# Cross-attention keys of a four-layer network on one core: K written once in fp32, split into two fp16 parts by GpSimd

## The reference, cut to what matters

```python
# ctx' : L1 ada_ln(ctx), L2 layer norm of ctx, L3 ctx itself
k = (ctx' @ Wk + bk)            # 1500 x 128, 16 heads of 8
v = (ctx' @ Wv + bv)
scores = einsum('bhqd,bhkd->bhqk', q, k) * 8 ** -0.5
out = einsum('bhqk,bhkd->bqhd', softmax(scores), v)
```

## Time and profile before

| | us |
|---|---|
| median of 3 runs (lowest, highest) | 2066.11 (2053.47, 2067.04) |
| profiled execution | 2056.51 |
| its span in the trace | 2054.7 |
| busy in the span: PE, DVE, ACT, POOL | 1635.4, 1236.0, 1004.1, 422.9 |

### The profile page before, as it was taken

One profiled execution on the slowest core, in us unless ns is written; L12 is line 12 of the kernel. 1 busy time (PEld: TensorE's weight loads), 2 busy tenths in 40 slices (PEclk: granted clock), 3 DMA queues, 4 the chain that ended last, 5 costly groups with the idle time before them and its releaser, 6 DMA issues.

```text
span 2054.7 us, 53923 instructions
## 1 busy us (share of the span) xinstructions
PE 1635.4 (80%) x20495; PEld 1030.7 (50%) x20495; DVE 1236.0 (60%) x2433; ACT 1004.1 (49%) x1911; POOL 422.9 (21%) x611
## 2 busy tenths in 40 slices
PE   4788777588887887787688888887785888888876
PEld 3465544255555555443355555555342455555554
DVE  5454443567775776364677777773364777777762
ACT  1243322166665666242366666663242466666662
POOL 7000133013331333135033333310131000000000
PEclk9798988599998998796699999996796799999997
DMA  5021122234443442040344444430040444444410
GB/s 174 26 77 64 45 44 62 55 82 112 112 110 94 113 102 73 1 103 3 72 112 113 111 109 111 110 98 14 0 102 11 92 116 117 114 114 112 106 43 9
DMA packets 178537, 166.32 MB, mean 81 GB/s; under 512 B 67551, under 2 KB 168098, under 8 KB 178402
## 3 DMA queue, kind: packets, MB, share of 16 engines
q1 hardware_dynamic: 176818, 163.35, 30.2%
q10 hardware_dynamic: 1008, 1.05, 0.2%
q0 software_dynamic: 576, 0.02, 0.0%
HBM read 114.46 MB, written 40.08 MB: 75 GB/s over the span
## 4 chain that ended last, share of the span: by engine, by line
PE 64%; issue 13%; DVE 10%; ACT 10%; DMA 1%; POOL 1%; ACTq 0%; DVEq 0%; SPq 0%; POOLq 0%
PE PS L1127 11%; PE PS L1022 8%; PE PS L1153 8%; PE PS L1016 8%; PE PS L862 6%; PE PS L1101 5%; PE PS L1011 3%; PE PS L941 3%; ACT q_parts L795 2%; DVE mx L1552 2%; PE PS L1227 2%; PE PS L959 2%; ACT v_sb L729 2%; ACT cxT L720 2%; PE PS L932 1%
## 5 line engine op out<-in xcount | busy, mean ns | idle before, releaser
L1552 DVE TENSOR_REDUCE mx<-PS 112x1 f32<-112x500 f32 x1152 | 718.4, 671 | 295.8 <-PE PS L1101 291.5
L795 ACT ACTIVATE q_parts<-PS 125x448 f32<-125x448 f32 x1152 | 562.2, 544 | 108.8 <-PE PS L1153 105.0
L585 POOL TENSOR_SCALAR cx<-cx,norm_b 125x128 f32<-125x128 f32 x384 | 303.5, 813 | 590.7 <-DMA cx<-in_ctx 488.2
L1153 PE MATMUL PS<-q_st,k_st 50*125 50x112 f16 x4608 | 263.1, 236 | 40.1 <-ACT q_parts L795 23.2
L1153 PEld LDWEIGHTS PS<-q_st,k_st 50*125 50x125 f16 x4608 | 186.4, 140 | 213.7 <-ACT q_parts L795 121.7
L1101 PE MATMUL PS<-k_st,q_mx 50*112 50x500 f16 x1152 | 262.5, 403 | 38.8 <-issue 24.2
L1127 PE MATMUL PS<-q_parts,v_sb 125*18 125x112 f32 x9216 | 291.4, 270 | 0.0
L1127 PEld LDWEIGHTS PS<-q_parts,v_sb 125*18 125x18 f32 x9216 | 218.4, 101 | 60.7 <-issue 52.1
L729 ACT ACTIVATE v_sb<-PS 125x512 f32<-125x512 f32 x144 | 87.1, 605 | 186.7 <-PE PS L1022 186.6
L725 ACT ACTIVATE k_hi<-PS,vec 128x500 f16<-128x500 f32 x144 | 97.5, 677 | 129.0 <-PE PS L1016 129.0
L1101 PEld LDWEIGHTS PS<-k_st,q_mx 50*112 50x112 f16 x1152 | 91.5, 133 | 74.5 <-issue 44.9
(11 more groups left out here) (266 smaller groups left out, 1994.1 us busy)
## 6 DMA issues: line engine op xcount, KB each, us to landing
k_st<-k_dram SPq DMA_DIRECT2D x864, 62.5 KB, 2.2
cx<-in_ctx SPq DMA_DIRECT2D x56, 750.0 KB
k_dram<-k_hi SPq DMA_DIRECT2D x144, 125.0 KB, 1.8
k_dram<-k_lo SPq DMA_DIRECT2D x144, 125.0 KB, 2.0
v_sb<-in_ctx SPq DMA_DIRECT2D x8, 750.0 KB
q_mx<-q_all SPq DMA_DIRECT2D x48, 99.8 KB
q_st<-q_all SPq DMA_DIRECT2D x48, 99.8 KB
q_all<-q_dram SPq DMA_DIRECT2D x18, 196.0 KB, 6.4
```

The source lines that it names most:

```text
L585: last = pool.tensor_scalar(cx[:, p, c, :], cx[:, p, c, :], norm_b[:, p, 0, c:c + 1], norm_b[:, p, 1, c:c + 1], ALU.subtract, ALU.mult)
L795: act.activation(probs[:, c % RING, u * HR:(u + 1) * HR], PS[0:KC, (2 * c + u) % SC_RING, 0:HR], ACT.Exp).then_inc(sem("exp_done"), 1)
L1153: last = mm(PS[0:KC, (2 * c + a) % SC_RING, k * PW:k * PW + PW], k_st[64 * a:64 * a + ROWS, p, k, c * KC:(c + 1) * KC], q_st[64 * a:64 * a ...
L1552: dve.tensor_reduce(mx[:, r, t:t + 1], PS[0:PW, MX_BANK + u % MX_RING, 0:TK], AX.X, ALU.max)\
```

## The change

RING goes from 6 to 4, and a new tile `k_full` (fp32, two buffers, by the parity of the batch) is added. ACT writes `k_full` with the bias, one instruction per K step as before, now behind `k_lo_done` of the batch two before. POOL makes both fp16 parts from it: a copy to `k_hi`, a wait for that copy, and a subtraction to `k_lo`. DVE's `k_low` is gone everywhere. PE's step behind a K step waits for `k_full_done` alone. POOL's `attend(b)` splits the keys of batch b+2 behind the normalisation of batch b+3; the keys of batches 0 and 1 are split by `split_first`, which for cross 2 and 3 stands behind all of the self attention's copies.

```diff
-RING = 6
+RING = 4
...
+        k_full = sb("k_full", [128, 2, S])
...
+            def split_keys(layer, batch, t):
+
+                b, i, p = batch
+                n = B * (layer - 1) + b
+                cols = slice(TK * t, TK * t + TK)
+                ge_known(pool, ("k_full_done", NT * n + t + 1), (f"k_out{t}", 32 * n))
+                pool.tensor_copy(k_hi[:, cols], k_full[:, p, cols]).then_inc(sem("k_hi_done"), 1)
+                ge_known(pool, ("k_hi_done", NT * n + t + 1))
+                pool.tensor_tensor(k_lo[:, cols], k_full[:, p, cols], k_hi[:, cols], ALU.subtract)\
+                    .then_inc(sem("k_lo_done"), 1)
+
+            def split_first(layer):
+                for b in range(2):
+                    for t in range(NT):
+                        split_keys(layer, (b, 0, b), t)
...
                     if third and cr["norm"] is not None:
                         copies(third)
                         normalise(third)
+                    if behind:
+                        for t in range(NT):
+                            split_keys(layer, behind, t)
...
+                split_first(1)
                 cross_copies(1, True)
             if layers > 2:
                 cross_copies(2, False)
                 self_copies(2)
+                split_first(2)
                 cross_copies(2, True)
             if layers > 3:
                 self_copies(3)
+                split_first(3)
                 cross_copies(3, True)
...
-                        ge(act, f"k_out{t}", 32 * n)
-                        act.activation(k_hi[:, TK * t:TK * t + TK], PS[:, bank, 0:TK], ACT.Identity, bias=cr["kb"])\
-                           .then_inc(sem("k_hi_done"), 1)
+                        ge(act, "k_lo_done", NT * (n - 2) + t + 1)
+                        act.activation(k_full[:, p, TK * t:TK * t + TK], PS[:, bank, 0:TK], ACT.Identity, bias=cr["kb"])\
+                           .then_inc(sem("k_full_done"), 1)
...
-                            pe.wait_ge(sem("k_hi_done"), NT * n + wt + 1)
-                            pe.wait_ge(sem("k_lo_done"), NT * n + wt + 1)
+                            pe.wait_ge(sem("k_full_done"), NT * n + wt + 1)
...
-                def k_low(batch, k, bank=MISC_BANK):
-                    kind, t = MISC[k]
-                    if kind != "K":
-                        return
-                    b, i, p = batch
-                    n = n0 + b
-                    dve.wait_ge(sem("k_hi_done"), NT * n + t + 1)
-                    ge(dve, f"k_out{t}", 32 * n)
-                    cols = slice(TK * t, TK * t + TK)
-                    dve.scalar_tensor_tensor(out=k_lo[:, cols], in0=PS[:, bank, 0:TK], scalar=cr["kb"],
-                                             in1=k_hi[:, cols], op0=ALU.add, op1=ALU.subtract)\
-                       .then_inc(sem("k_lo_done"), 1)
...
-                        of_next, k = SLOT_MISC.get(c - 1, (True, None))
-                        if behind and not of_next:
-                            k_low(behind, k)
```

More of the change, by code:

```diff
@@ L1444, in l0_last @@
                 l0_evidence(b)
-            def preparation(layer):
-                cr = cross_of(layer)
-                n0 = B * cr["n"]
-                def k_low(batch, k, bank=MISC_BANK):
-                    kind, t = MISC[k]
-                    if kind != "K":
-                        return
-                    b, i, p = batch
-                    n = n0 + b
-                    dve.wait_ge(sem("k_hi_done"), NT * n + t + 1)
-                    ge(dve, f"k_out{t}", 32 * n)
-                    cols = slice(TK * t, TK * t + TK)
-                    dve.scalar_tensor_tensor(out=k_lo[:, cols], in0=PS[:, bank, 0:TK], scalar=cr["kb"],
-                                             in1=k_hi[:, cols], op0=ALU.add, op1=ALU.subtract)\
-                       .then_inc(sem("k_lo_done"), 1)
-                return k_low
             l0_batches(l0_first, l0_both, l0_last, dve)
@@ L1471, in _ @@
             dve.tensor_copy(halves(A[5]), pair(0)).then_inc(sem("evid_done"), 1)
-            k_low = preparation(1)
             for e in range(E):
@@ L1493, in _ @@
             for k in range(2 * E + 1):
-                if layers > 1:
-                    ahead(k_low, AHEAD[3 * k:3 * k + 1], DENSE_BANK)
                 dve.wait_ge(sem("hid_tanh"), k + 1)
@@ L1502, in _ @@
                                          op0=ALU.add, op1=ALU.mult).then_inc(sem("hid_done"), 1)
-                if layers > 1:
-                    ahead(k_low, AHEAD[3 * k + 1:3 * k + 3], DENSE_BANK)
                 if k == 1:
@@ L1544, in cross @@
                     last.then_inc(sem("q_split"), 1)
-                k_low = preparation(layer)
                 def unit(batch, u):
@@ L1675, in both @@
                     front(n)
-                    ahead(k_low, beside[0:1], SELF_BANK)
                     back(b)
-                    ahead(k_low, beside[1:3], SELF_BANK)
                 batches(dve, front, both, back)
```

## The result

The changed kernel takes 2178.87 us (median of 4 runs, 2167.86 to 2186.88), the kernel before 2062.36 us beside it. The ratio is 1.0567, with a 95% interval of 1.0499 to 1.0635: slower by 5 to 6%. Forecast were 2153 us and slower. The profiled execution has a span of 2183.1 us, 128.4 more than before. The page of the profile after: the span, the busy times, the chain of waits by engine, and the groups that answer to the earlier trace rows (busy us, mean ns | idle before and its releaser).

A forecast was written before the change was run, and what follows sets the result against it. PE, the busiest engine, was taken to wait for DVE's `k_lo`. The terms 67 + 78 - 41 - 10 + 2.5 = +96.5 us on 2054.7 gave 2151.2, with 1.8 around it 2153; 8-in-10 range 2095 to 2220.

The forecast's parts named there:

- The unnamed wait: PE's wait before the K and V projections, taken as the one for `k_lo_done`: 2.96 us per key-preparing attend.
- The closed ring: Crosses 1 and 2: load, normalisation, split, `k_out`, next load in sequence, 33.55 us per round against 25.4; +67 and +78 us.
- The split's two estimates: POOL's copy and two-input subtraction of 128 x 500 per t: 0.65 and 0.94 us, 1.9 per split with semaphore waits.
- some 10 us of idle time before the first unit: Sign of being right: PE idle some 10 us before L1101 of each attend in crosses 1 and 2.
- rival 5: PE's clock falls as PE idles about 11 us per batch; near its lower level throughout, 2373 us; chance 0.04.
- What is late next is PE itself ... I take the full 41 us: Cross 3: with the `k_lo` waits gone PE itself limits, saving 41 us; bound 0 if another wait takes its place.
- The boundary before cross 3: `split_first` behind POOL's last self-attention copies keeps SP busy, so q is 2.5 us late (0 to 8).
- the 10 in all: Same waits vanishing in the dense part and the self attentions: 10 us saved (0 to 16).
- 1 (open ring): The wait goes and POOL and SP keep pace because loads land early enough: 1925 us; chance 0.06.
- 2: The ring closes but PE's waits stay, through another semaphore or an equal wait: 2210 us; chance 0.06.
- 3: POOL's new instructions cost what `tensor_scalar` costs, 6.7 us per split and 41.4 per round: 2325 us; chance 0.04.
- 4: Round 2 us shorter because loads find quieter queues: 2109 us; part of the forecast's own range, no separate chance.

The follow-up runs named there:

- dve_split: Kernel before with RING = 4, ACT writing `k_full`, PE waiting for ACT alone, and DVE instead of POOL making `k_hi` and `k_lo`: 1953.79 us, ratio 0.9473.
- no_load3: Changed kernel without the context loads of batches 4 to 15 in cross 3: 2158.53 us, ratio 1.0471; cross 3 takes 334.8 us.
- act_load3: Changed kernel with cross 3's context loads of batches 4 to 15 issued by ACT's queue instead of SP: 2197.90 us, ratio 1.0646.
- early_first: Changed kernel with the load ahead of the keys and, before crosses 2 and 3, batches 0 and 1 split between POOL's self-attention copies: 1974.20 us, ratio 0.9561.
- load_early: Changed kernel with SP issuing load(b+4) ahead of `k_out` 0 of batch b+2, no longer behind `k_out` 2: 1993.18 us, ratio 0.9647.

## Why the prediction was right

**The unnamed wait was `k_lo_done`.** Shown twice: `dve_split` changes nothing on POOL and SP and loses the waits with 109 us, and the changed kernel's lists of cross 2 and cross 3 have none before L1038 and L1044 (over its whole span 12.4 us are left there, 0.9 of them unnamed).

**The closed ring, by its terms.** Forecast 10.7 + 9.35 + 1.9 + 0.1 + 11.5 = 33.55; measured 10.4, 9.3, 1.9, 0.1 and 11.6, 33.4 to 33.7 per round. The split's two estimates were 0.65 and 0.94; they measured 0.61 and 1.14, with the waits between them smaller than the 0.3 allowed. The Trainium skill (GPSIMD Engine Reference, Performance versus the Vector engine) gives 2.6 cycles per element for such a two-input operation, by which 1.08 us before dispatch is the estimate, and the trace, with 1.14, is nearer to it than to my 0.94 from the row of 896 columns. Crosses 1 and 2 came to +71.1 and +82.0 where 67 and 78 were forecast. Three runs show cause and not only size: moving the load (-186 us), moving the split (-156 us), and shortening the normalisation by 4.7 us, which gave 3.5 and 4.4 per round.

**What PE did meanwhile.** I forecast some 10 us of idle time before the first unit of each attend. In cross 2 it is 4.2 to 6.4 us there in the attends of the ring, with shorter waits before unit 16, 83.4 us in 23 waits in all, and PE is busy 410 us of 510 at a granted clock of 0.80; in the kernel before, 989 to 1417 us, it was 366 of 428 at 0.92. Part of the slack went into a lower clock instead of into idle time. As rival 5's caveat had it, this did not reach the ring.

**Where the sum was off.** The span rose by 128.4 us, not 96.5. Some 12 of it may be chance in which executions were profiled: the profiled one of before is 6 us under its median, that of after 6 us over, and the medians differ by 116.5. Of the 31.9 us between the spans, 8 are in crosses 1 and 2, 18 in cross 3, and 6 in the rest.
- The step that failed is "What is late next is PE itself ... I take the full 41 us". Cross 3 gave 22.8. The waits went as forecast, but what was late next was not PE alone: at 22 us per attend `k_st` comes late behind the 750 KB load (up to 10.0 us from issue to landing), PE waits 11.3 us for keys, and it is busy 330.9 us at a granted clock of 0.96 where it was busy 325.4 at 0.99. The clock fell during the two longest of these waits, and these two attends take 30 us. `no_load3` gives 22 us back, and `act_load3` shows that the place on SP's queue is not the cause; that the bytes are is argued from what is left. I had named 0 as the lower bound, "if another wait takes its place", and should have priced that wait from SP's row: a chain of `k_out`, `k_in`, load and q loads of about 20 us in a period that was to shrink to 22.
- The boundary before cross 3 was forecast at 2.5 us. From the linear step of q to the first shift it took 10.1 us longer: 5.5 because SP came late (I had 2.5 for this), and 4.4 because q's write then landed behind 18 transfers and a load, which I had not counted. `early_first` takes this back.
- The dense part gave 11.5 us and the self attention before cross 2 3.4, more than the 10 in all; that before cross 3 gave nothing (10.6 us longer, 10.1 of them the boundary), and the end took 2.5 us longer.

**The rivals.** 1 (open ring) did not occur as built, but is what `load_early` makes of it: 1993, not 1925, mainly since none of its crosses goes below 360 us. 2 is excluded by the lists of waits. 3 is excluded by 609 and 1140 ns. 4, a round 2 us shorter, did not come: 10.4 for the load where 10.7 were taken, and the round as forecast. 5 occurred as a lower clock, without a price in crosses 1 and 2, where the ring is longer than PE's work, and with some 8 us in cross 3, where PE is on the path.

**What stays open.** `dve_split` needs 355.5 us for cross 3 with hardly a wait for `k_st`; PE is busy 335.3 us of it, and 321.5 in `no_load3` at the same clock of 0.99. The waits for DVE's maxima are 6.1 us. Of the 14 us by which it is busy longer, the trace puts 12.2 on one line, the products of the row maxima (L1101, 85.05 us against 72.84, with the same median of 373 ns for one), whose instructions wait for DVE's maxima too. So the difference points at DVE's longer work, but no run tests it. Nor was it tried why cross 1 stays over cross 2 when the ring is open. How the load delays the keys (the DMA engines, DRAM, or both) was not told apart either.

## What to carry to other kernels

Before work is moved to an idle engine, follow what that engine's program has ahead of it, and whether this in turn waits for something issued behind the moved work: a circle through two in-order queues costs the sum of its latencies in every iteration, however idle its engines are. The repair is often a move of a line or two: here a load issued ahead of the keys made a kernel 8.5% faster than the one with the same work in the other order. And when a stall is removed, price the next wait at the new period, transfers included: here a wait of 3 to 5 us on the busiest engine cost some 4 us more through its clock.

## What the runs showed of the hardware that was not expected

A transfer from another queue did not help a crowded one: with the 750 KB loads on ACT's queue, SP's issue times fell (q_mx from 38.0 to 14.7 us in 16), but its waits for landing in DRAM rose from 57.3 to 105.1 us and cross 3 got no shorter. And a write that landed 2.0 us after its issue took 6.4 us when 18 transfers of 62.5 KB and a load stood ahead of it on its queue. Single waits of PE came with a lower clock: in cross 3 of the changed kernel it went to 1.2 GHz during waits of 5.0 and 2.9 us, stayed there for 10.2 us each time, and was at 2.4 GHz in the nine attends behind the second. The work of each of the two attends took PE 4.1 us more than in `no_load3`.
